# Local attention: dividing the softmax weights before they are transposed

## The reference

```python
def _layer(x, wqkv, qs, ksc, wo, lg, lb, w1, b1, w2, b2):   # run 2 layers x 2 calls
    qkv = shift_token(x) @ wqkv                # 3 x 512 columns: 8 heads of 64
    q, k = rotary_xpos(l2norm(q) * qs, l2norm(k) * ksc)
    # windows of 64 queries see their own and the previous window: 128 keys
    sim = jnp.einsum('bhwid,bhwjd->bhwij', 8 * bq, bk)   # masked
    attn = jax.nn.softmax(sim, axis=-1)
    o = jnp.einsum('bhwij,bhwjd->bhwid', attn, bv)
    x = x + o @ wo
    h = layernorm(shift_token(x)) * lg + lb
    a, g = jnp.split(h @ w1 + b1, 2, axis=-1)
    return x + (a * gelu(g)) @ w2 + b2
```

## Time and profile before

| what | value |
|---|---|
| median of three runs | 1274.42 us (1271.28 to 1274.9) |
| profiled execution, its own time | 1284.16 us |
| its span, first to last instruction | 1282.4 us |
| mean granted TensorE clock | 0.933 of full speed |
| busy: TensorE / VectorE / ScalarE / GpSimd | 1061.7 / 798.1 / 703.6 / 390.2 us |

### The profile page before, as it was taken

The page is one execution under the profiler, slowest core; times in us unless marked ns, Lnnn a source line. Parts: engine busy times, 40 slices in busy tenths (PEclk is TensorE's granted clock), DMA queues, the critical chain, the costliest instruction groups (busy, mean ns, idle before and its releaser), DMA issues.

```text
span 1282.4 us, 21857 instructions
## 1 busy us (share of the span) xinstructions
PE 1061.7 (83%) x8144; PEld 654.8 (51%) x8144; DVE 798.1 (62%) x1381; ACT 703.6 (55%) x1500; POOL 390.2 (30%) x251
## 2 busy tenths in 40 slices
PE   4079984079985789999899898989898998998996
PEld 2023332023333666667666665656565666666662
DVE  4088824078825667658668666667677676776652
ACT  3037752027762566646656565656566475575662
POOL 4000014000004654343543334242435334344330
PEclk9589997579997899999999999999999999999998
DMA  2950002930003010001000000000000010101100
GB/s 64 127 95 8 1 1 68 97 50 2 1 1 87 22 26 17 19 18 23 22 19 22 18 14 18 14 17 14 18 14 22 18 23 18 22 13 34 30 10 17
DMA packets 38267, 35.99 MB, mean 28 GB/s; under 512 B 11478, under 2 KB 30224, under 8 KB 38160
## 3 DMA queue, kind: packets, MB, share of 16 engines
q1 hardware_dynamic: 34708, 31.46, 13.6%
q10 hardware_dynamic: 3456, 3.15, 1.2%
HBM read 15.41 MB, written 4.21 MB: 15 GB/s over the span
## 4 chain that ended last, share of the span: by engine, by line
PE 35%; DVE 11%; ACT 9%; POOL 8%; issue 6%; POOLq 0%; DVEq 0%; ACTq 0%
PE psum L1076 8%; PE psum L1164 6%; PE psum L1137 5%; ACT f_PW L1271 5%; POOL f_A L976 4%; PE psum L1052 3%; PE psum L1087 2%; POOL f_A L971 2%; DVE f_A L1390 2%; DVE f_NM L1422 2%; DVE f_BS L1394 2%; PE psum L1099 2%; POOL f_HL L963 2%; PE psum L1061 2%; DVE f_SS L1401 1%
## 5 line engine op out<-in xcount | busy, mean ns | idle before, releaser
L1271 ACT ACTIVATE f_PW<-psum,f_NM 128x128 f32<-128x128 f32 x512 | 139.3, 383 | 169.1 <-DVE f_NM L1422 169.1
L976 POOL TENSOR_TENSOR f_A<-f_A,f_RN 128x1024 f32<-128x1024 f32 x64 | 121.8, 1902 | 290.0 <-ACT f_RN L1282 288.7
L500 DVE TENSOR_REDUCE a_M<-psum 128x1 f32<-128x512 f32 x256 | 159.9, 683 | 71.1 <-PE psum L430 70.7
L430 PE MATMUL psum<-a_KS,a_QS 128*128 128x512 bf16 x256 | 103.7, 414 | 79.8 <-DMA a_KS<-minus_ones 76.7
L971 POOL TENSOR_TENSOR f_A<-f_A,f_BS 128x1024 f32<-128x1024 f32 x64 | 151.2, 2362 | 48.9 <-DVE f_BS L1394 47.4
L547 ACT ACTIVATE a_PT<-psum 128x1024 f32<-128x1024 f32 x128 | 126.4, 1018 | 56.8 <-PE psum L452 56.5
L1390 DVE TENSOR_TENSOR f_A<-psum,cos 128x512 f32<-128x512 f32 x128 | 87.7, 686 | 93.7 <-ACT f_SQ L1239 93.7
L1422 DVE TENSOR_REDUCE f_NM<-psum 128x4 f32<-128x512 f32 x128 | 82.4, 685 | 78.0 <-PE psum L1076 78.0
L1076 PE MATMUL psum<-f_KT,f_QT 64*64 64x128 f32 x2048 | 129.5, 277 | 1.5
L1076 PEld LDWEIGHTS psum<-f_KT,f_QT 64*64 64x64 f32 x2048 | 113.8, 136 | 30.3 <-issue 19.2
L1052 PE MATMUL psum<-const,f_A 128*128 128x128 f32 x512 | 72.4, 288 | 45.5 <-POOL f_A L976 45.5
(11 more groups left out here) (173 smaller groups left out, 1900.0 us busy)
## 6 DMA issues: line engine op xcount, KB each, us to landing
f_VS<-f_V SPq DMA_DIRECT2D x112, 130.0 KB, 2.3
parts<-a_PRT ACTq DMA_DIRECT2D x24, 128.0 KB, 2.4
a_QS<-parts SPq DMA_DIRECT2D x8, 256.0 KB
a_KS<-parts SPq DMA_DIRECT2D x8, 256.0 KB
a_QS<-parts SPq DMA_DIRECT2D x4, 384.0 KB
a_KS<-parts SPq DMA_DIRECT2D x4, 384.0 KB
raw<-L_ffn_wqkv_dram SPq DMA_DIRECT2D x2, 768.0 KB, 7.0
a_XT<-L_attn_a_x_dram SPq DMA_DIRECT2D x4, 256.0 KB, 4.1
```

Of the source, the lines that this page charges most:

```text
L430: nc.tensor.matmul(psum[:, take("tile", 8 * unit + k), :], QS[:, n, h + k // 4, P * qt:P * qt + P], KS[:, n, h + k // 4, :], start=True, s ...
L500: nc.vector.tensor_reduce(M[:, u % 4, k // 4, k % 4:k % 4 + 1], psum[:, bank("tile", i), :], AX_X, ALU.max)\
L976: nc.gpsimd.tensor_tensor(x, x, RN[:, k % 2, :, None].to_broadcast([P, 2 * HW, DW]), ALU.mult)\
L1271: last = nc.scalar.activation(PW[:, u % 4, c, :], psum[:, bank("scores", u), P * c:P * c + P], ACT.Exp, bias=NM[:, u % 4, c:c + 1])
```

## The change

The weights are summed and divided before they are transposed. A new stage `weigh` of tile k-1 stands after `scale` of tile k and before `sums` of k-2. In it VectorE waits for the exponentials of each window, reduces PW (128x512) to four sums and takes their reciprocal; GpSimd then multiplies PW by it. `turn_p` waits for that (`weighed`). `sums` takes the values as the stationary side and PT as the moving one, so that the result stands by feature, both windows in one bank; ScalarE copies it to OT in stage `sums`. `turn_o`, ON, the division and the columns of ones are gone; wo's weights are loaded in their natural order, by one DMA a layer for four. The waits that counted `sums` by window count it by tile.

```diff
-        tile(step - 3, "turn_o")
...
         tile(step, "scale")
+        tile(step - 1, "weigh")
         tile(step - 2, "sums")
...
-             "sums": ("divided", lambda i: i + 1), "turn_o": ("o_copied", lambda i: i + 1),
+             "sums": ("o_copied", lambda i: i + 1),
...
+                    elif stage == "weigh":
+                        for u in (2 * i, 2 * i + 1):
+                            pool.wait_ge(s("den_recip"), u + 1)
+                            nc.gpsimd.tensor_tensor(PW[:, u % 4, :, :], PW[:, u % 4, :, :],
+                                                    RR[:, u % 4, :, None].to_broadcast([P, PAIRS, P]), ALU.mult)\
+                                .then_inc(s("weighed"), 1)
...
                 def turn_p(k):
                     for u in (2 * k, 2 * k + 1):
-                        pe.wait_ge(s("exped"), u + 1)
+                        pe.wait_ge(s("weighed"), u + 1)
...
-                        dst = take("sums", u)[:, 0:PAIRS * (DW + 1)].rearrange("p (c x) -> p c x", c=PAIRS)
+                        if w == 0:
+                            dst = take("sums", k).rearrange("p (c x) -> p c x", c=PAIRS)
                         for c in range(PAIRS):
                             for j in range(2):
                                 last = nc.tensor.matmul(
-                                    dst[WIN * j:WIN * j + WIN, c, :], PT[:, u % 4, c, WIN * j:WIN * j + WIN],
-                                    values[:, k % 4, 2 * c + j, :], start=True, stop=True)
-                        last.then_inc(s("sums"), 1)
+                                    dst[DW * j:DW * j + DW, c, WIN * w:WIN * w + WIN], values[:, k % 4, 2 * c + j, :],
+                                    PT[:, u % 4, c, WIN * j:WIN * j + WIN], start=True, stop=True)
+                    last.then_inc(s("sums"), 1)
...
-                    elif stage == "turn_o":
+                    elif stage == "sums":
                         k = i
                         m, t = k // TILES, k % TILES
-                        act.wait_ge(s("turned_o"), k + 1)
+                        act.wait_ge(s("sums"), k + 1)
...
-                    elif stage == "sums":
+                    elif stage == "weigh":
                         for u in (2 * i, 2 * i + 1):
-                            x = psum[:, bank("sums", u), 0:PAIRS * (DW + 1)].rearrange("p (c x) -> p c x", c=PAIRS)
-                            dve.wait_ge(s("sums"), u + 1)
-                            nc.vector.reciprocal(RD[:, u % 4, :], x[:, :, DW]).then_inc(s("den_recip"), 1)
-                            dve.wait_ge(s("den_recip"), u + 1)
+                            dve.wait_ge(s("exped"), u + 1)
+                            nc.vector.tensor_reduce(RD[:, u % 4, :], PW[:, u % 4, :, :], AX_X, ALU.add)\
+                              .then_inc(s("den"), 1)
+                            dve.wait_ge(s("den"), u + 1)
                             if u >= 4:
-                                dve.wait_ge(s("turned_o"), u // 2 - 1)
-                            nc.vector.tensor_tensor(ON[:, u % 4, :, :], x[:, :, 0:DW],
-                                                    RD[:, u % 4, :, None].to_broadcast([P, PAIRS, DW]), ALU.mult)\
-                              .then_inc(s("divided"), 1)
+                                dve.wait_ge(s("weighed"), u - 3)
+                            nc.vector.reciprocal(RR[:, u % 4, :], RD[:, u % 4, :]).then_inc(s("den_recip"), 1)
```

More of the change, by code:

```diff
@@ L803, in stream @@
             order += [("turned_q", i), ("turned_k", i)]
-        elif stage in ("turn_p", "scores", "sums", "keys_b", "tokens_b"):
+        elif stage in ("turn_p", "scores", "keys_b", "tokens_b"):
             order += [(stage, 2 * i), (stage, 2 * i + 1)]
@@ L809, in stream @@
             order += [("latent", i), ("query_b", i)]
-        elif stage in ("turn_o", "wo", "center", "var", "w2", "context", "features_b", "project_b", "store"):
+        elif stage in ("sums", "wo", "center", "var", "w2", "context", "features_b", "project_b", "store"):
             order += [(stage, i)]
@@ L894, in row @@
                     return a[name][layer:layer + 1]
-                by_head = row("L0_ffn_wo").rearrange("a (cc c j d) n -> c d (a cc) j n", cc=2, c=2, j=2)
                 todo += [
-                    *((wo[DW * c:DW * c + DW, layer, 2 * cc:2 * cc + 2, :], by_head[c, :, cc])
-                      for c in range(2) for cc in range(2)),
+                    (wo[:, layer, :, :], row("L0_ffn_wo").rearrange("a (c p) n -> p (a c) n", p=P)),
                     (w1[:, layer, :], row("L0_ffn_w1").rearrange("a p n -> (a p) n")),
@@ L928, in _ @@
                         if k >= 4:
-                            sp.wait_ge(s("sums"), 2 * k - 6)
+                            sp.wait_ge(s("sums"), k - 3)
                         sp.dma_start(VS[WIN:P, k % 4, :, :], V[0:WIN, k % 4, :, :]).then_inc(s(f"moved{k % 4}"), 16)
@@ L1099, in sums @@
                                 last = nc.tensor.matmul(
-                                    dst[WIN * j:WIN * j + WIN, c, :], PT[:, u % 4, c, WIN * j:WIN * j + WIN],
-                                    values[:, k % 4, 2 * c + j, :], start=True, stop=True)
-                        last.then_inc(s("sums"), 1)
-                def turn_o(k):
-                    dst = take("turn_o", k).rearrange("p (cc j w q) -> p cc j w q", cc=2, j=2, w=2)
-                    for w in range(2):
-                        u = 2 * k + w
-                        pe.wait_ge(s("divided"), u + 1)
-                        for cc in range(2):
-                            last = nc.tensor.transpose(dst[:, cc, :, w, :],
-                                                       ON[:, u % 4, 2 * cc:2 * cc + 2, :].rearrange("p c d -> p (c d)"),
-                                                       g.ident)
-                    last.then_inc(s("turned_o"), 1)
-                pe.wait_ge(s("zeroed"), 3)
+                                    dst[DW * j:DW * j + DW, c, WIN * w:WIN * w + WIN], values[:, k % 4, 2 * c + j, :],
+                                    PT[:, u % 4, c, WIN * j:WIN * j + WIN], start=True, stop=True)
+                    last.then_inc(s("sums"), 1)
+                pe.wait_ge(s("zeroed"), 2)
                 for stage, i in plan:
@@ L1287, in _ @@
                         if u >= 4:
-                            act.wait_ge(s("sums"), u - 3)
+                            act.wait_ge(s("sums"), i - 1)
                         nc.scalar.activation(PT[:, u % 4, :, :],
@@ L1298, in _ @@
                         nc.scalar.activation(OT[:, :, P * t:P * t + P],
-                                             psum[:, bank("turn_o", k), :].rearrange("p (c x) -> p c x", c=PAIRS),
+                                             psum[:, bank("sums", k), :].rearrange("p (c x) -> p c x", c=PAIRS),
                                              ACT.Copy).then_inc(s("o_copied"), 1)
@@ L1412, in _ @@
                         if u >= 4:
-                            dve.wait_ge(s("sums"), u - 3)
+                            dve.wait_ge(s("sums"), i - 1)
                         nc.vector.tensor_copy(PT[:, u % 4, :, :],
```

15 lines of the change are left out of this document (5 added, 10 removed).

## The result

| | before | after |
|---|---|---|
| median, four runs each on one chip | 1273.16 us | 1318.38 us |
| ratio, 95% interval | | 1.0363 [1.0326, 1.0401] |
| profiled execution: time / span | 1284.16 / 1282.4 us | 1316.79 / 1315.0 us |
| mean granted TensorE clock | 0.933 | 0.918 |

The change costs 45.2 us. Slower was forecast, but by 27.9 us: 1302, with a range to 1316, and 1318 lies outside it.

The account below looks back on a forecast made before the run. No single engine was taken as the bound (TensorE 83% busy), but waits through VectorE, GpSimd and TensorE, read per step. Step terms, filling and draining summed to 27.9 us slower, added to the median: 1302 us, range 1284 to 1316.

Parts of the forecast that it names:

- Wo step after a `low_part`: ScalarE's later work delays rope, Y, GpSimd and the transposes of A by 0.5 us, 8 times: 4.0 us slower.
- ScalarE's order: OT's copy moves ahead of ScalarE's squares, so rope and all behind it begins 0.5 us later.
- Storing w2 steps: Three w2 steps that store: L971 ends 0.95 us later, X by as much, 2.8 us slower in all.
- The second attention: Four periods with the second attention, 1.2 us slower each over norm, gate, w2 and wo steps: 4.8 us.
- in wo and norm steps that wait eats the gain whole: Removing four transposes a tile (0.44 us) gains nothing there, because TensorE then waits for A.
- The norm step: Twelve norm steps outside the second attention: L971 and then L1405 end later, maxima 0.92 us later each, 11.0 us.
- The gate step: Twelve gate steps outside the second attention: `hidden` is later and frees a bank later, scores 0.35 us later each, 4.2 us.
- The multiply's price: GpSimd's added multiply of 128x512 takes 1.03 us, between 0.95 and 1.264.
- the multiplies are hidden: Rival: under 0.8 us a GpSimd multiply, only ScalarE's 0.5 us remains; 13.6 us slower, 1288; 20 in 100.
- a multiply costs as L999: Rival: each GpSimd multiply takes 0.23 us more, some 13 us more in norm and gate steps, 1315; 14 in 100.
- VectorE's cover is gone: Rival: reduction and reciprocal end 0.5 us later, rope up to 0.4 later; some 8 us more, 1310; 10 in 100.
- The second attention's wo steps: Wo steps in the four second-attention periods become 0.8 us shorter: 0.44 and 0.86 ahead of the wait, less ScalarE's 0.5.

Follow-up runs that it names:

- e1: Changed kernel with two extra 512-column matmuls in TensorE's idle time ahead of the transposes of A in wo steps and ahead of three stores: 1314.32 us, ratio 1.0296.
- e12: As e9, without the extra matmuls ahead of the second attention's norm-step scores and of the transposes of A in tiles 25, 29, 33, 37: 1295.14 us, 1.0145.
- e13: Kernel before with extra matmuls in the wo steps as in e12 and, in the second attention, ahead of `k` and the masks: 1273.73 us, ratio 0.999.
- e5: Changed kernel without VectorE's maximum with `tiny`, 1e-24 added inside ScalarE's logarithm instead: 1290.06 us, ratio 1.0105.
- e4: Changed kernel with ScalarE's copy of OT back at its old place, a step later behind V's copy: 1305.61 us, ratio 1.0230.
- e3: Changed kernel without GpSimd's two multiplies of PW; reductions, reciprocals and the new place of OT's copy stay: 1304.83 us, ratio 1.0191.
- e2: Kernel before with the same two extra matmuls as e1: 1283.72 us, ratio 1.0059.
- e9: As e1 on the changed kernel, with more extra matmuls in the second attention, ahead of `v`, the scores' second bank and `center`: 1303.46 us, ratio 1.0219.

## Why the prediction was wrong in size and right in direction

*The step that failed.* The sum priced each wait by its length and every TensorE instruction by its duration in a row of before. So "Wo step after a `low_part`, 8 times: the 0.5 of ScalarE's order", 4.0 us, took TensorE's matmuls in that step as they are in the earlier trace rows; and "Storing w2 steps ... L971 later by 0.95, X by as much", 2.8 us, took the scores behind X as they are in the earlier trace rows. The runs showed in their place: nine wo steps 10.4 us longer, all of it gone in e1, and stores 2.4 each, of which e1 leaves 0.77. The second attention got 14.2 longer for 4.8; in e12 it is 4.3 above before. So the step that failed is the price of TensorE's work behind a wait: it was taken at full clock, and it ran at a granted clock of 0.50. Together, e12 is 16.1 us above before in the stretch where the changed kernel is 43.4 above. Part of this before would have gained as well: e12 is 21.8 us above e13, and 26.1 above a kernel that takes its second attention from before and the rest from e13. So some 17 to 22 of the 43.4 us came with the clock (13 if the estimate under e13 holds). Nor is the clock the only handle: without the maximum 29 of the 43.4 us go (e5), with no idle time filled. The prediction had no rival for this, though the page had the mean clock (0.933), and the four wo steps of before with 14.6 to 14.8 us for 13.06 could have been read from its trace: one has `wo` at 4.29 us.

```profile
1017.17 4.29 PE L1137 MATMUL psum<-f_OT,f_wo 128*128 128x512 f32 x8
```

*What made the idle time longer.* The two edits that were booked as nothing or little: the four transposes of ON left the queue ahead of the wait ("in wo and norm steps that wait eats the gain whole": 0.44 us that TensorE now stands idle instead), and ScalarE's copy delays rope and `low_part` by 0.48. Idle 2.76 us in the earlier trace rows became 3.46 in the step at 608.54. e4 takes away the second part alone; the idle time is 3.31 to 3.34 then, so most of the growth isn't the copy's, and the 0.44 of the transposes is the larger part of it. Yet 13 us of time go with the copy, more than its own term.

*The norm step* was 0.92 and is 0.68; it is counted 11 times and not 12. The chain is the forecast one, but L966 starts 0.79 later and not 0.95 (the multiplies overlap by some hundredths, 2.04 for two), and 0.1 of it was slack: before, f_mid began 0.14 us behind the end of the copy of PT (1132.13 + 0.68), with ScalarE's f_LR (1132.28 + 0.63); after, 0.04. e5 confirms that both ends are equally near: without the maximum the step is no shorter.

*The gate step* was 0.35 and is 0.52; e5 (12.90) shows that the maximum sets it, and e3 that 0.23 of it remains without the multiplies.

*ScalarE's order* was 0.5 and is 0.48, shown by e4; it lies in the distance that ends in the wo step's multiply, 7 times outside the filling.

*The multiply's price* held: 1036 to 1043 ns for all 128, for 1.03. The rivals "the multiplies are hidden" and "a multiply costs as L999" fall by this row. "VectorE's cover is gone" falls too: VectorE is still idle ahead of rope in the norm step, 0.49 us at 1207.14.

*The second attention's wo steps* were to be 0.8 us shorter. With the clock up (e12) they are 19.14 for 21.40, 2.3 shorter. How much of this is the order of work isn't shown: before, these steps had a low clock too (0.72 from 912 to 918). The wait for Y isn't gone either; it stands behind `v`'s matmuls now, 3.11 us at 910.21. As the changed kernel ran, two of its wo steps had lost all of it (22.53 and 22.52).

*By the sum as a whole*: 27.9 was forecast, and with idle times filled the change costs 22 to 26 us (30 by the estimate under e13). So the sum without the clock isn't shown to be too dear. The filled changed kernel (e12) ran in 1295 us, inside the range.

*Open.* Which idle time lowers the clock I can't say: before, TensorE stood idle 2.76 or 2.77 us ahead of the transposes of A in seven wo steps; in three of them `wo` ran at 1.00, in four not. After, it was idle 3.42 to 3.47 in the same seven, and none ran at 1.00 throughout. The tail behind the last multiply with RN took 46.2 us before and 44.6 in e13, which drains alike, so its term (-1.9 forecast, -3.4 in the one profile) isn't settled. That the extra matmuls act through the clock alone rests on the granted clock of the windows and the unchanged end of the wait; an idle time filled by anything else wasn't tried.

## What to carry to other kernels

Read, before any sum, whether the same line has two durations in the trace of before, and what TensorE did ahead of the longer one: a wait there costs its length and the slower matmuls behind it. Then work taken from TensorE ahead of a wait is no gain and can be a loss, and a few idle matmuls put inside a wait (not behind one) can give back as much as a shorter chain: 23 us in e12, 28 in e5. Read from the trace whether they really stand inside it: in e2, e9 and e13 some did not. Price an instruction moved to GpSimd together with the VectorE instructions that read two SBUF inputs and fall beside it.

## What the runs showed of the hardware that was not expected

- Behind idle times of 3.46 and 2.34 us, eight transposes took 1.97 us for 1.09, 32 matmuls of scores 3.62 for 1.96, and `wo`'s eight 5.63 for 3.60, at a granted clock of 0.50 over the transposes and 0.53 over the scores, for 1.00. With two matmuls of 512 columns put into the idle time they took 1.09, 1.96 and 3.60 again. The Trainium skill ("TensorE: Matmul & The Clock Gate", HAM oscillation — how this bites in real kernels) tells of a kernel whose matmuls start slow again behind each wait for a transfer; these runs agree in part: 1.97 us for 1.09 behind a wait for GpSimd, but not behind each wait of the same length (2.77 us at 1015.41, 2.76 in the earlier trace rows).
- VectorE with two SBUF inputs is held by GpSimd in both sizes seen: 0.17 us became up to 1.62 for 128x16, and 0.69 became 1.46 for 128x512. The reduction from SBUF (1.207 to 1.214 us in all 64) wasn't.
- The same multiply on VectorE, 1.18 us in the mean, was dearer than on GpSimd with its 1.04.
